# Second attention of a two-attention transformer block: the value product as three float16 matmuls with a lag of two steps

## The chip, the cores and the metric

The kernel runs on one core of one Trainium2 chip. The metric is device microseconds of one execution, as the median of repeated runs. TensorE is called PE here, its weight loads PEld, VectorE DVE, ScalarE ACT, GpSimd POOL.

## The reference, cut to what matters

A sequence of 2048 tokens with 128 channels passes through an attention with 16 heads of 64, a feed-forward block, a second attention with 8 heads of 128 (rotary positions, causal mask) and a second feed-forward block, each behind a layer norm and added to the stream. The change is in the second attention:

```
q = _rope(einsum('btm,mhd->bthd', x, w_aq));  k = _rope(einsum(..., w_ak));  v = einsum(..., w_av)
s = einsum('bihd,bjhd->bhij', q, k) / 128 - 1e30 * mask        # mask: i < j
p = softmax(s, axis=-1)
o = einsum('bhij,bjhd->bihd', p, v)
r = einsum('bihd,hdm->bim', o, w_ao)
```

## The kernel before

Every engine has a program of its own, written out by hand; semaphores tie them. An engine works strictly in its own order, so the order of each program sets everything.

**The second attention.** For each of the 8 heads, queries are taken in 4 units of 512 (qb = 0 to 3; below, unit 0 to unit 3). Unit qb has 4(qb+1) steps of 128 keys, so a head has 4 + 8 + 12 + 16 = 40 steps. The last four steps of a unit lie on the diagonal and have 512, 384, 256 and 128 query columns. Two heads make one turn of a loop; the first and the last turn are written out.

**One step on PE** (`body_b`): three matmuls of keys by queries with 512 columns (L1459, L1461, L1463; high and low parts of q and k) onto a PSUM bank that ACT has filled with minus the row maximum; then a first ring item; then `pv_b` of the step before: up to four value products (query tiles 0 and 1, a second ring item, query tiles 2 and 3), each one float32 matmul of 129 columns (128 values and a column of ones, L1436); then the remaining ring items. The score banks are two, `SB[step % 2]`.

**Ring items** are all other PE work: two PSUM banks `RING`, used in turn. PE may write item n only when DVE has taken item n-2 (`claim`). Kinds: `max` (a score matmul for the row maximum of a later unit, L1389, taken by DVE with a reduction, L855), `rows` and `spread` (bring the maxima into place), `project` (q or k of the next head, L1369; DVE takes it with three multiplications, L1021 to L1023), `values` (V of the next head, L1377; DVE copies it, L1040), `turned` (transpose of the normalised output of the unit before, L1206) and `output` (its product with the output weights, L1214). In unit 3 a `project` stands in steps 1, 3, 5 and 8; in unit 1 in step 5; in unit 2 in steps 3, 6 and 9. In unit 2, steps 0 to 7 have two `max` items each, and `values` stand in steps 4, 7 and 10.

**ACT** per step: wait for the scores, exponential into `PRB` (L719), copy minus the maxima into the score bank for step + 2 (`fill`, L700); one step after a `project`, the rounded high part of q or k (L689), which waits for POOL's sum.

**POOL**: for each `project` a sum (`rope_sum_b`, L512) once DVE has taken it, then the low part (`low_b`, L519) once ACT has the high part. Otherwise it is idle here.

**DVE**: takes ring items in their order; in step 1 of a unit, ahead of that step's items, it normalises the unit before (`normalise_b`, L1030 to L1034), which needs that unit's last value product. `turned` in step 2 waits on PE for this (`o_taken`).

The first attention has the same skeleton; its value products are already pairs of 16-bit matmuls of 194 and 130 columns (L1247, L1248) whose low part of P is made by POOL (L449).

## Time and profile before

| | |
|---|---|
| three runs | 2596.69, 2598.87, 2598.98 us (median 2598.87) |
| span of the profiled execution | 2594.6 us; the page gives no other time for it |
| mean granted PE clock over the span | 0.975 |
| first attention, about | 55 to 1725 us of the span |
| second attention | 1827 to 2547 us, 720 us, 90 us a head |
| busy share over the span | PE 92%, PEld 73%, DVE 68%, ACT 67%, POOL 57% |

How to read it: the span runs from the first to the last instruction of the profiled execution. A matmul's record ends with its modelled pipeline, well after the next one has started. What PE spends on a matmul is therefore read from one start to the next, not from its duration, and PE's busy share hides short waits.

### The profile page before, as it was taken

To read this page: it belongs to the slowest core of one execution; us is meant where nothing else is said; L and a number is where in the kernel's file an instruction comes from. 1 tells how busy PE (TensorE), PEld (TensorE's weight loads), DVE (VectorE), ACT (ScalarE), POOL (GpSimd) and SP (SyncE) were. 2 spreads that over 40 slices of the span, in tenths; PEclk is the share of its full clock that TensorE was granted. 3 is DMA by queue.
4 is the path that set the end of the run, shared out by engine and by line. 5 is a ranking of instruction groups with operands and counts; after the bars stand their busy time and mean duration, and the time that the engine had idled before them with its cause. 6 is when DMAs were issued, how large, how long until landed. Compare 5 with 4: busy or idle time off the path is not lost.

```text
span 2594.6 us, 47816 instructions
## 1 busy us (share of the span) xinstructions
PE 2390.6 (92%) x17315; PEld 1882.8 (73%) x17315; DVE 1769.3 (68%) x3012; ACT 1732.4 (67%) x2190; POOL 1469.7 (57%) x826
## 2 busy tenths in 40 slices
PE   5999999999899899989989999977899999999998
PEld 3777777677777677767767777754788887888786
DVE  6777767677677677767776777666666665666652
ACT  4877877778688687777878878752455454455554
POOL 5787777677687677767777777753122112122200
PEclk7999999999999999999999999988899999999999
DMA  3000000000000000000000000010000000000000
GB/s 94 1 1 1 1 1 1 2 1 1 2 1 1 2 1 1 2 2 1 1 2 1 1 1 1 1 41 1 1 1 1 1 1 2 1 1 1 1 1 17
DMA packets 15276, 13.06 MB, mean 5 GB/s; under 512 B 3120, under 2 KB 14384, under 8 KB 14768
## 3 DMA queue, kind: packets, MB, share of 16 engines
q1 hardware_dynamic: 15024, 9.72, 1.4%
q8 instruction: 156, 2.56, 0.4%
q14 instruction: 96, 0.79, 0.1%
HBM read 8.67 MB, written 1.05 MB: 4 GB/s over the span
## 4 chain that ended last, share of the span: by engine, by line
PE 46%; issue 26%; DVE 13%; POOL 9%; ACT 4%; SPq 0%; DMA 0%; DVEq 0%; POOLq 0%; ACTq 0%
PE OO L1247 6%; PE RING L1193 6%; PE ST L1297 5%; POOL PAB L449 5%; PE ST L1298 5%; DVE maxes L855 4%; PE OO L1248 4%; PE OO L1436 3%; DVE OSUM L889 2%; PE RING L1214 2%; POOL F L512 2%; PE RING L1173 2%; PE RING L1389 1%; PE ST L1459 1%; ACT PAB L636 1%
## 5 line engine op out<-in xcount | busy, mean ns | idle before, releaser
L449 POOL TENSOR_TENSOR PAB<-PR,PAB 128x1024 f16<-128x1024 f32 x512 | 1093.2, 2137 | 407.8 <-ACT PAB L636 390.1
L855 DVE TENSOR_REDUCE maxes<-RING 128x1 f32<-128x512 f32 (+1 forms) x1344 | 883.9, 670 | 417.4 <-PE RING L1193 294.1
L634 ACT ACTIVATE PR<-ST,lift 128x1024 f32<-128x1024 f32 x512 | 569.1, 1111 | 360.0 <-PE ST L1298 354.0
L1247 PE MATMUL OO<-VP,PAB 128*128 128x194 bf16 x4096 | 688.3, 250 | 5.5 <-POOL PAB L449 2.0
L1248 PE MATMUL OO<-VP,PAB 128*128 128x130 bf16 x4096 | 653.3, 220 | 0.0
L636 ACT ACTIVATE PAB<-ST,lift 128x1024 f16<-128x1024 f32 x512 | 565.8, 1105 | 0.0
L1247 PEld LDWEIGHTS OO<-VP,PAB 128*128 128x128 f16 x4096 | 400.7, 98 | 190.4 <-issue 127.1
L1193 PE MATMUL RING<-KH,QL 128*128 128x512 f32 x1024 | 457.0, 453 | 46.4 <-DVE maxes L855 39.7
L1297 PE MATMUL ST<-QL,KH 128*128 128x512 f32 x1024 | 453.9, 443 | 29.2 <-issue 13.7
L1248 PEld LDWEIGHTS OO<-VP,PAB 128*128 128x128 f16 x4096 | 403.7, 99 | 10.8 <-issue 9.9
L1298 PE MATMUL ST<-QH,KL 128*128 128x512 f32 x1024 | 405.6, 396 | 0.0
L512 POOL TENSOR_TENSOR F<-F,PR 128x512 f32<-128x512 f32 x64 | 81.4, 1272 | 508.9 <-DVE PR L1023 508.9
L719 ACT ACTIVATE PR<-ST 128x512 f32<-128x512 f32 (+1 forms) x320 | 169.4, 529 | 260.5 <-PE ST L1463 258.5
L1193 PEld LDWEIGHTS RING<-KH,QL 128*128 128x128 f32 x1024 | 196.1, 192 | 139.0 <-DVE maxes L855 117.8
L1436 PEld LDWEIGHTS OO<-PAB,PR 128*128 128x128 f32 x1536 | 227.4, 192 | 41.1 <-issue 22.7
L1436 PE MATMUL OO<-PAB,PR 128*128 128x129 f32 x1536 | 250.7, 280 | 0.0
L1297 PEld LDWEIGHTS ST<-QL,KH 128*128 128x128 f32 x1024 | 195.5, 191 | 66.4 <-issue 38.7
L1298 PEld LDWEIGHTS ST<-QH,KL 128*128 128x128 f32 x1024 | 195.9, 191 | 33.0 <-issue 7.2
L700 ACT ACTIVATE ST<-VF 128x512 f32<-128x512 f32 (+1 forms) x320 | 172.0, 538 | 26.7 <-PE ST L1425 15.3
L1459 PE MATMUL ST<-QH,KH 128*128 128x512 f32 (+1 forms) x320 | 146.3, 457 | 1.0
L1389 PE MATMUL RING<-KH,QH 128*128 128x512 f32 (+2 forms) x320 | 129.3, 408 | 14.7 <-ACT PR L719 8.1
L831 DVE TENSOR_TENSOR KL<-F,KH 64x512 fp32r<-64x512 f32 x64 | 120.5, 1882 | 24.5 <-ACT KH L594 24.0
(132 smaller groups left out, 3044.4 us busy)
## 6 DMA issues: line engine op xcount, KB each, us to landing
X<-in_L_attn_a_x SPq DMA_DIRECT2D x4, 256.0 KB, 4.3
SHARED<-in_rope_cos SPq DMA_DIRECT2D x1, 1024.0 KB, 4.9
SHARED<-in_rope_sin SPq DMA_DIRECT2D x1, 1024.0 KB, 7.1
out<-X SPq DMA_DIRECT2D x4, 256.0 KB, 2.3
RAW<-in_L_attn_a_Wq SPq DMA_DIRECT2D x1, 512.0 KB, 7.5
RAW<-in_L_attn_a_Wk SPq DMA_DIRECT2D x1, 512.0 KB, 7.8
RAW<-in_L_attn_a_Wv SPq DMA_DIRECT2D x1, 512.0 KB, 5.7
RAW<-in_L_attn_a_Wo SPq DMA_DIRECT2D x1, 512.0 KB, 6.8
```

The lines of the kernel that those rows point to most:

```text
L449: pool.tensor_tensor(PB[:, s, :], PR[:, step % 2, :], PA[:, s, :], ALU.subtract).then_inc(p_low_pool, 1)
L634: act.activation(PR[:, step % 2, :], ST[step % 2][:, :], ACT.Exp, bias=lift[:, :])
L636: act.activation(PA[:, step % SLOTS_A, :], ST[step % 2][:, :], ACT.Exp, bias=lift[:, :]).then_inc(sa.exps, 1)
L700: act.activation(SB[parity][:, c0:BLK], MB[:, slot, c0:BLK], ACT.Copy).then_inc(sbb.filled, 1)
L855: dve.reduce_max(maxes[:, qt, c:c + 1], bank[:, 0:width], X_AXIS).then_inc(s.ring_taken, 1)
L1193: pe.matmul(bank[:, :], QL[hs][:, at:at + P], KH[hs][:, c * BLK:(c + 1) * BLK], start=True, stop=True).then_inc(sa.ring_put, 1)
L1247: pe.matmul(o, high, v, start=(m == 0 and qt % 2 == 0), stop=False, skip_group_check=True)
L1248: ins = pe.matmul(o[:, 0:V3_AT], low, v[:, 0:V3_AT], start=False, stop=(m == TILES - 1), skip_group_check=True)
L1297: pe.matmul(tile, KH[hs][:, keys], QL[hs][:, q], start=True, stop=False)
L1298: ins = pe.matmul(tile, KL[hs][:, keys], QH[hs][:, q], start=False, stop=True)
L1436: ins = pe.matmul(bank[:, at:at + VB], PRB[:, step % 2, qt * P:(qt + 1) * P], VBS[:, ul // BLOCKS, step, :], start=(step == 0 and qt in (0 ...
L1459: pe.matmul(tile, KH[hs][:, keys], QH[hs][:, q], start=False, stop=False, skip_group_check=True)
```

## The change

P and V are each split into a float16 high part and a float16 low part, and one float32 value product becomes three float16 matmuls: P high by V high (129 columns), P high by V low (128), P low by V high (129). ACT computes the exponential twice, once in float32 (`PRB`) and once in float16 (`PBH`, four slots). POOL subtracts the two to get the low part (`p_low_part`). `pv_b` now runs two steps behind the scores, and waits for POOL. With it, DVE's `normalise_b` moves from step 1 to step 2 of a unit, while `turned` stays in step 2. DVE takes `values` with two operations, the second waiting for the first. In POOL's program `low_b` of a `project` stands two steps later, ahead of that step's `p_low_part`. Outside the second attention: V is scaled by a power of two from a bound on its size (two POOL products and two DVE sums at the head of the first attention, a chain of seven small DVE operations and one product on POOL behind it), and the maxima are raised by a constant. Cut to its core:

```diff
@@ -73,6 +74,9 @@
 VB = DB + 1
+VSTEP = DB + 2
+SLOTS_B = 4
+LAG_B = 2
 ITER_B = HB // 2
@@ -154,11 +159,13 @@
             items += [("rows", target)]
-    if not (first and ul == 0):
-        items += [("turned",)] if step == 2 else [("output",)] if step == 3 else []
+    if step == LAG_B + 1 and not (first and ul == 0):
+        items += [("output",)]
     if next_head:
         items += [("project", b) for b in PROJECT_B.get((qb, step), [])]
         items += [("values", VALUES_B[qb, step])] if (qb, step) in VALUES_B else []
+    if step == LAG_B and not (first and ul == 0):
+        items += [("turned",)]
     return items
@@ -524,21 +552,36 @@
                     low_b(0, j, j)
+            pool.wait_ge(vscale_ready, 2)
+            pool.tensor_scalar(WAO, WAO, vdown[:, 0:1], None, ALU.mult).then_inc(ones_set, 1)
             pool.wait_ge(x_ready, BLOCKS)
-            pool.memset(VBS[:, :, :, DB:VB], 1.0).then_inc(ones_set, 1)
+            pool.memset(VBH[:, :, :, DB:VB], 1.0).then_inc(ones_set, 1)
+
+            def p_low_part(step, c0, g):
+
+                pool.wait_ge(sbb.exps, g + 1)
+                wait(pool, sbb.pv, g - SLOTS_B + 1)
+                s = step % SLOTS_B
+                pool.tensor_tensor(PBL[:, s, c0:BLK], PRB[:, step % 2, c0:BLK], PBH[:, s, c0:BLK], ALU.subtract
+                                   ).then_inc(p_low_b, 1)
             def heads_b(it, first=False, last=False):
                 k = SKIP if first else 0
+                g = it * G_B
                 for ul in range(UNITS_B):
                     hs, qb = divmod(ul, BLOCKS)
                     head = it * 2 + hs + 1
                     if qb == 0 and not (last and hs == 1):
                         stage_b(1 - hs, head)
                     for step in range(steps_b(qb)):
+                        for item in ring_items_b(ul, step - 2, first, last) if step >= 2 else []:
+                            if item[0] == "project":
+                                low_b(1 - hs, item[1], head * 2 * BLOCKS + item[1])
+                        p_low_part(step, max(0, step - BT * qb) * P, g)
+                        g = g + 1
                         for item in ring_items_b(ul, step, first, last):
                             if item[0] == "project":
                                 rope_sum_b(item[1], LEAD_B - SKIP + it * RING_B + k)
-                                low_b(1 - hs, item[1], head * 2 * BLOCKS + item[1])
                             k += 1
@@ -715,8 +758,11 @@
                         act.wait_ge(sbb.scores, g + 1)
-                        wait(act, sbb.pv, g - 1)
+                        wait(act, p_low_b, g - 1)
                         act.activation(PRB[:, step % 2, c0:BLK], SB[step % 2][:, c0:BLK], ACT.Exp,
+                                       scale=1.0 / DB)
+                        wait(act, sbb.pv, g - SLOTS_B + 1)
+                        act.activation(PBH[:, step % SLOTS_B, c0:BLK], SB[step % 2][:, c0:BLK], ACT.Exp,
                                        scale=1.0 / DB).then_inc(sbb.exps, 1)
@@ -856,9 +903,10 @@
                     link(dve.tensor_reduce(negmax[:, :], maxes[:, :, 0:chunks], X_AXIS, ALU.max, negate=True))
-                    link(dve.tensor_copy(negparts[:, 0:BT].bitcast(F32R), negmax[:, :]))
-                    dve.tensor_tensor(negparts[:, BT:AUX], negmax[:, :], negparts[:, 0:BT],
-                                      ALU.subtract).then_inc(s.max_ready, 1)
+                    raised = LIFT_B if s is sbb else 0.0
+                    link(dve.tensor_scalar(negparts[:, 0:BT].bitcast(F32R), negmax[:, :], raised, None, ALU.add))
+                    dve.scalar_tensor_tensor(negparts[:, BT:AUX], negmax[:, :], raised, negparts[:, 0:BT],
+                                             ALU.add, ALU.subtract).then_inc(s.max_ready, 1)
@@ -1002,6 +1053,17 @@
             normalise_settled(7)
+            dve.wait_ge(vtotal_put, 1)
+            link(dve.tensor_copy(vbound[:, :], O[1][:, 0:2]))
+            link(dve.tensor_tensor(vbound[:, 0:1], vbound[:, 0:1], vbound[:, 1:2], ALU.add))
+            link(dve.tensor_scalar(vbound[:, 0:1], vbound[:, 0:1], float(P), 1e-30, ALU.mult, ALU.max))
+            link(dve.tensor_scalar(vexp[:, :].bitcast(I32), vbound[:, 0:1].bitcast(I32), 1, 0x7F800000,
+                                   ALU.arith_shift_right, ALU.bitwise_and))
+            dve.tensor_scalar(vup[:, :].bitcast(I32), vexp[:, :].bitcast(I32), -1.0, float(204 << 23),
+                              ALU.mult, ALU.add).then_inc(vscale_ready, 1)
+            dve.tensor_scalar(vdown[:, :].bitcast(I32), vexp[:, :].bitcast(I32), 1.0, float(50 << 23),
+                              ALU.mult, ALU.add).then_inc(vscale_ready, 1)
+            dve.wait_ge(vscale_ready, 2)
@@ -1037,8 +1099,11 @@
                 dve.wait_ge(sbb.ring_put, item + 1)
-                dve.tensor_copy(VBS[:, hs, part * BT:(part + 1) * BT, 0:DB],
-                                bank[:, :].rearrange("p (t c) -> p t c", c=DB)).then_inc(sbb.ring_taken, 1)
+                v = bank[:, :].rearrange("p (t c) -> p t c", c=DB)
+                high = VBH[:, hs, part * BT:(part + 1) * BT, 0:DB]
+                link(dve.tensor_scalar(high, v, vup[:, 0:1], None, ALU.mult))
+                dve.scalar_tensor_tensor(VBL[:, hs, part * BT:(part + 1) * BT, :], v, vup[:, 0:1], high,
+                                         ALU.mult, ALU.subtract).then_inc(sbb.ring_taken, 1)
@@ -1082,7 +1147,7 @@
                     for step in range(steps_b(qb)):
-                        if step == 1 and not (first and ul == 0):
+                        if step == LAG_B and not (first and ul == 0):
                             normalise_b((ul - 1) % UNITS_B, done)
@@ -1424,17 +1492,22 @@
             ins.then_inc(sbb.primed, 1)
-            pe.wait_ge(ones_set, 2)
+            pe.wait_ge(ones_set, 3)
             def pv_b(ul, step, g, half):
                 qb = ul % BLOCKS
+                hs = ul // BLOCKS
                 if half == 0:
-                    pe.wait_ge(sbb.exps, g + 1)
+                    pe.wait_ge(p_low_b, g + 1)
                 for qt in range(max(2 * half, step - BT * qb), 2 * half + 2):
                     bank, at = (OB[ul % 2][0], qt * VB) if qt < 3 else (OB[ul % 2][1], 0)
-                    ins = pe.matmul(bank[:, at:at + VB], PRB[:, step % 2, qt * P:(qt + 1) * P],
-                                    VBS[:, ul // BLOCKS, step, :], start=(step == 0 and qt in (0, 3)),
+                    high, low = (p[:, step % SLOTS_B, qt * P:(qt + 1) * P] for p in (PBH, PBL))
+                    pe.matmul(bank[:, at:at + VB], high, VBH[:, hs, step, 0:VB],
+                              start=(step == 0 and qt in (0, 3)), stop=False, skip_group_check=True)
+                    pe.matmul(bank[:, at:at + DB], high, VBL[:, hs, step, :], start=False, stop=False,
+                              skip_group_check=True)
+                    ins = pe.matmul(bank[:, at:at + VB], low, VBH[:, hs, step, 0:VB], start=False,
                                     stop=(step == BT * qb + qt), skip_group_check=True)
@@ -1493,14 +1566,14 @@
                         ring_items(1)
-                        if not (first and ul == 0 and step == 0):
-                            pul = ul if step else (ul - 1) % UNITS_B
-                            pstep = step - 1 if step else steps_b(pul % BLOCKS) - 1
-                            if step == 1:
+                        if not (first and ul == 0 and step < LAG_B):
+                            pul = ul if step >= LAG_B else (ul - 1) % UNITS_B
+                            pstep = step - LAG_B if step >= LAG_B else steps_b(pul % BLOCKS) + step - LAG_B
+                            if step == LAG_B:
                                 wait(pe, sbb.o_taken, u - 1)
-                            pv_b(pul, pstep, g - 1, 0)
+                            pv_b(pul, pstep, g - LAG_B, 0)
                             ring_items(1)
-                            pv_b(pul, pstep, g - 1, 1)
+                            pv_b(pul, pstep, g - LAG_B, 1)
                         ring_items(len(items) - place)
```

How rows move, at the start of unit 3 of the first head. On PE, before, from the `project` of step 1 (L1369) to the end of step 2. L1436 into OO or ST1 is a value product, L1459 to L1463 are the scores, L1388 and L1389 the `max`, L1206 `turned`:

```order
L1369 MATMUL RING1<-XNT,WST 128x512
L1436 MATMUL OO<-PAB,PR 128x129 x3
L1436 MATMUL ST1<-PAB,PR 128x129
L1459 MATMUL ST0<-QH0,KH0 128x512
L1461 MATMUL ST0<-QH0,KL0 128x512
L1463 MATMUL ST0<-QL0,KH0 128x512
L1388 MATMUL RING0<-later_keys,ident_r 128x128
L1389 MATMUL RING0<-KH1,QH1 128x128
L1436 MATMUL OO<-PAB,PR 128x129 x2
L1206 MATMUL RING1<-ident,AB 128x128 x4
```

and after, the same place from the `project` (L1437) on. L1506, L1508, L1510 are one value product, L1532 to L1536 the scores, L1456 and L1457 the `max`:

```order
L1437 MATMUL RING1<-XNT,WST 128x512
L1506 MATMUL ST1<-PAB,VP 128x129
L1508 MATMUL ST1<-PAB,VP 128x128
L1510 MATMUL ST1<-PAB,VP 128x129
L1532 MATMUL ST0<-QH0,KH0 128x512
L1534 MATMUL ST0<-QH0,KL0 128x512
L1536 MATMUL ST0<-QL0,KH0 128x512
L1456 MATMUL RING0<-later_keys,ident_r 128x128
L1457 MATMUL RING0<-KH1,QH1 128x128
```

The last value product of unit 2 (into ST1), which stood ahead of the scores of step 1, now stands behind them and behind the `project`. Two value products and `turned` (now L1271) follow as before.

On DVE, at the same place, before: `values` (L1040), `normalise_b` (L1030 to L1034), the `project` of step 1, `max`, `turned` (L872):

```order
L1040 COPY PAB<-RING1 128x4x128
L1030 RECIPROCAL rden<-OO 128x3
L1031 RECIPROCAL rden<-ST1 128x1
L1032 TENSOR_TENSOR AB<-OO,rden 128x384
L1034 TENSOR_SCALAR AB<-ST1,rden 128x128
L1021 TENSOR_TENSOR F<-RING1,SHARED 128x512
L1022 TENSOR_TENSOR PR<-RING1,SHARED 64x512
L1023 TENSOR_TENSOR PR<-RING1,SHARED 64x512
L855 TENSOR_REDUCE maxes<-RING0 128x1
L872 COPY AT<-RING1 128x512
```

and after:

```order
L1104 TENSOR_SCALAR PAB<-RING0,vup 128x4x128
L1105 SCALAR_TENSOR_TENSOR PAB<-RING0,vup,PAB 128x512
L1083 TENSOR_TENSOR F<-RING1,SHARED 128x512
L1084 TENSOR_TENSOR PR<-RING1,SHARED 64x512
L1085 TENSOR_TENSOR PR<-RING1,SHARED 64x512
L1092 RECIPROCAL rden<-OO 128x3
L1093 RECIPROCAL rden<-ST1 128x1
L1094 TENSOR_TENSOR AB<-OO,rden 128x384
L1096 TENSOR_SCALAR AB<-ST1,rden 128x128
L902 TENSOR_REDUCE maxes<-RING0 128x1
L920 COPY AT<-RING1 128x512
```

The normalisation now stands behind the `project` instead of ahead of it, and `values` are two operations.

## Rows read from the trace of the kernel before

**Rows 1.** Stretch, length, busy us of PE, PEld, DVE, ACT, POOL, clock, DMA share, GB/s.

```profile
100.00:1690.00 1590.00, 1495.49 (x11692) 1148.07 (x11692) 1145.98 (x1724) 1234.54 (x1320) 1202.39 (x618) 0.99 0.01 1
1827.00:2547.00 720.00, 687.62 (x4456) 589.34 (x4455) 450.45 (x857) 370.43 (x694) 146.37 (x124) 0.99 0.00 1
```

**Rows 2.** PE timeline, second attention: start, duration (us), operation, count; two records a product.

```profile
2000.47 0.83 PE L1436 MATMUL OO<-PAB,PR 128*128 128x129 f32 x6
2001.14 0.39 PE L1436 MATMUL ST<-PAB,PR 128*128 128x129 f32 x2
2001.29 0.47 PE L1459 MATMUL ST<-QH,KH 128*128 128x512 f32 x1
2001.60 0.39 PE L1461 MATMUL ST<-QH,KL 128*128 128x512 f32 x1
2001.82 0.39 PE L1463 MATMUL ST<-QL,KH 128*128 128x512 f32 x1
```

**Rows 3.** PE timeline, first attention: pairs of 16-bit matmuls around a score matmul.

```profile
1200.11 0.25 PE L1247 MATMUL OO<-VP,PAB 128*128 128x194 bf16 x1
1200.20 0.22 PE L1248 MATMUL OO<-VP,PAB 128*128 128x130 bf16 x1
1200.25 0.25 PE L1247 MATMUL OO<-VP,PAB 128*128 128x194 bf16 x1
1200.34 0.22 PE L1248 MATMUL OO<-VP,PAB 128*128 128x130 bf16 x1
1200.37 0.47 PE L1193 MATMUL RING<-KH,QL 128*128 128x512 f32 x1
1200.68 0.26 PE L1247 MATMUL OO<-VP,PAB 128*128 128x194 bf16 x1
```

**Rows 4.** DVE timeline, unit 3, start: normalisation, taking the `project`, `max`.

```profile
1976.64 0.18 DVE L1030 RECIPROCAL rden<-OO 128x3 f32<-128x3 f32 x1 [2.03 <-PE ST L1436]
1977.38 0.34 DVE L1034 TENSOR_SCALAR AB<-ST,rden 128x128 f32<-128x128 f32 x1
1978.60 0.69 DVE L1021 TENSOR_TENSOR F<-RING,SHARED 128x512 f32<-128x512 f32 x1 [0.87 <-PE RING L1369]
1980.72 0.29 DVE L855 TENSOR_REDUCE maxes<-RING 128x1 f32<-128x128 f32 x1
```

**Rows 5.** PE timeline, same stretch: `project` and `turned`.

```profile
1977.54 1.02 PE L1369 MATMUL RING<-XNT,WST 128*128 128x512 f32 x2
1980.75 0.66 PE L1206 MATMUL RING<-ident,AB 128*128 128x128 f32 x4
```

**Rows 6.** ACT timeline where a `project` is followed by short steps (idle before, releaser).

```profile
1944.06 0.63 ACT L689 ACTIVATE QH<-F 128x512 fp32r<-128x512 f32 x1 [1.57 <-POOL F L512]
1945.43 0.58 ACT L719 ACTIVATE PR<-ST 128x512 f32<-128x512 f32 x1
1946.04 0.60 ACT L700 ACTIVATE ST<-VF 128x512 f32<-128x512 f32 x1
1946.58 0.58 ACT L719 ACTIVATE PR<-ST 128x512 f32<-128x512 f32 x1
```

**Rows 7.** PE timeline, unit 2: the second `max` behind a `project`.

```profile
1956.34 0.50 PE L1389 MATMUL RING<-KH,QH 128*128 128x512 f32 x1 [0.82 <-DVE PR L1023]
```

**Rows 8.** POOL groups: low part of P, first attention; sum, second attention (busy us, mean ns).

```profile
L449 POOL TENSOR_TENSOR PAB<-PR,PAB 128x1024 f16<-128x1024 f32 x486 | 1037.8, 2137 | 386.8 <-ACT PAB L636 369.3 <-PE OO L1248 17.4
L512 POOL TENSOR_TENSOR F<-F,PR 128x512 f32<-128x512 f32 x52 | 66.2, 1274 | 405.7 <-DVE PR L1023 405.7
```

**Rows 9.** DVE groups: `values` in the second attention; L860 in first, then second attention.

```profile
L1040 DVE COPY PAB<-RING 128x512 f32<-128x512 f32 x25 | 17.3, 692 | 8.1 <-PE RING L1377 7.6
L860 DVE TENSOR_TENSOR negparts<-negmax,negparts 128x4 f32<-128x4 f32 x61 | 53.5, 878 | 2.1
L860 DVE TENSOR_TENSOR negparts<-negmax,negparts 128x4 f32<-128x4 f32 x27 | 4.4, 163 | 0.9
```

**Rows 10.** The page's group of 16-bit weight loads, first attention (busy us, mean ns).

```profile
L1248 PEld LDWEIGHTS OO<-VP,PAB 128*128 128x128 f16 x4096 | 403.7, 99 | 10.8 <-issue 9.9
```

More of the change, by code:

```diff
@@ L87 @@
 AUX = 2 * BT
+LIFT_B = DB * float(np.log(LIFT))
 def steps_b(qb):
@@ L232, in build @@
         rden = sb("rden", [P, BT])
+        ones_f = sb("ones_f", [P, P])
+        vsum = sb("vsum", [P, 2])
+        vbound = sb("vbound", [P, 2])
+        vexp = sb("vexp", [P, 1])
+        vup = sb("vup", [P, 1])
+        vdown = sb("vdown", [P, 1])
         KH = [sb(f"KH{i}", [P, T], F32R) for i in range(2)]
@@ L298, in build @@
         wt_put = sem("wt_put")
+        squared = sem("squared")
+        vsum_ready = sem("vsum_ready")
+        vtotal_put = sem("vtotal_put")
+        vscale_ready = sem("vscale_ready")
+        p_low_b = sem("p_low_b")
         wt_act = sem("wt_act")
@@ L1324, in _ @@
             output(sa, RING[(END_A - 1) % 2], END_A - 1, WoT[:, ITER_A - 1, :])
+            pe.wait_ge(vsum_ready, 1)
+            pe.matmul(O[1][:, 0:2], ones_f[:, :], vsum[:, :], start=True, stop=True).then_inc(vtotal_put, 1)
             pe.wait_ge(sa.ring_taken, END_A)
@@ L1511, in _ @@
             k = body_b(ITER_B - 1, last=True)
-            for half in range(2):
-                pv_b(UNITS_B - 1, TILES - 1, ITER_B * G_B - 1, half)
+            for step in range(TILES - LAG_B, TILES):
+                for half in range(2):
+                    pv_b(UNITS_B - 1, step, ITER_B * G_B - TILES + step, half)
             n = LEAD_B - SKIP + (ITER_B - 1) * RING_B + k
```

19 lines of the change are left out of this document (17 added, 2 removed).

## The prediction

> **What bounds the kernel now.** I began with the busy time by stretch. In the second attention, 720 of the 2594.6 us, PE is busy 687.6 us, DVE 450, ACT 370 and POOL 146 [rows 1]: PE is nearly full and POOL, where the new work goes, is nearly empty. That speaks for the change. But a matmul's record ends late, so PE's busy time hides short waits, and I read PE's timeline from start to start. Three value products take 2001.14 - 2000.47 = 0.67 us, 0.223 us each; a score matmul takes 0.22 to 0.23 us [rows 2]. A full step is then 3 x 0.227 + 4 x 0.223 = 1.57 us plus ring items. With all items so counted (`project` 0.86 us from [rows 5] to the next start; `turned`, `output` and `values` by the same float32 rate of 0.11 us for 128 columns), a head comes to about 83 us, where the trace has 720 / 8 = 90 [rows 1]. So some 7 us a head are already waits, in three kinds: PE for DVE behind a `project` (0.82 us in [rows 7]); ACT for POOL's sum (1.57 us in [rows 6]) and PE then for ACT; and the turn of the loop. PE waits there for an order, not for throughput, and a faster product shortens none of it.
>
> **The products.** The program of the changed kernel has 136 products a head, 1088 in all. The nearest row for the new kind is the first attention's pair of 194 and 130 columns, 0.14 us from start to start (1200.11 to 1200.25), of which the 130 columns take 0.05 to 0.06 (1200.20 to 1200.25) [rows 3]. Three of 129, 128 and 129 columns come to 3 x 0.057 = 0.171 us. Saved: 0.052 x 1088 = 56.6 us. Against it stands the end of each run of such matmuls: the float32 score matmul behind it takes 1200.68 - 1200.37 = 0.31 us and the last 16-bit one 0.03, together 0.34 where 0.057 + 0.227 = 0.284 would be due: 0.06 lost [rows 3]. Before, the same place costs nothing: the last record of a product begins at about 2001.26, the second next score matmul at 2001.60, 0.34 us for 0.11 + 0.23 [rows 2]. A ring item splits the products of most steps, so there are 58 runs a head, 464: 27.8 us lost. Net for PE: **-28.7 us**. Bounds: -56.6 if the loss vanishes; the other end is the rival on weight loads below.
>
> **The transpose that waits.** `normalise_b` moves to step 2, and `turned`, which needs it, stays there. Worked out at unit 3 of the profiled head. PE begins the `project` of step 1 at 1977.54 [rows 5] and would be through with it at 1978.40, with the one product behind it (0.23) at 1978.63, the scores of step 2 (0.68) at 1979.31, the `max` (0.29) at 1979.60, two products (0.40) at 1980.0: there `turned` is due. DVE takes the `project` from 1978.60 to 1980.7, and only then normalises, which took 1976.64 to 1977.72, 1.08 us [rows 4]: 1981.8. `turned` waits 1.8 us; before it began at 1980.75 [rows 5] with no wait for the normalisation, which was over. I take 1.7. In unit 1, DVE still has two `max` of 0.69 when step 2 begins, then 1.08, then the `max` whose bank `turned` needs: 0.9 us of wait, 0.7 more than now. In units 0 and 2 the same count gives 0.5 and 0.3. While PE waits, all that stands behind it waits: the remaining products, the scores of step 3 and so ACT and POOL. 1.5 us in eight heads and 1.7 in seven (the last head has no `project`): **+23.5 us**. Bounds: 0 if DVE runs ahead everywhere, 30 if all four waits are as in unit 3's arithmetic without overlap.
>
> **ACT.** Each step gets a second exponential. From exponential to fill 0.61 us, from fill to the next exponential 0.54 (1945.43, 1946.04, 1946.58) [rows 6]; two exponentials in a row overlap, so a full step costs 0.54 + 0.61 + 0.54 = 1.69 us. Where ring items stand, PE needs 1.6 to 2.9, and ACT hides. In the last head's unit 3 there are none: PE would need 0.68 + 4 x 0.171 + 0.06 = 1.42, ACT 1.69 for 12 steps: the 1.7 us counted as saved there are not, and 0.7 come on top: +2.4. The last two products of all then wait for two exponentials and POOL: +0.8. Behind the `project` of unit 1 the steps are short and ACT, held by POOL's sum until 1944.06 [rows 6], then has 1.69 us of work a step to catch up with instead of 1.15; but the lag of two gives 1.1 us back. +0.2 a head, 1.5. Together **+4.7**.
>
> **POOL.** 512 columns of `p_low_part` cost half of 2137 ns, 1.07 us; the two operations for a `project` 1.27 each [rows 8]. In unit 3, steps 3 to 7, POOL has five of the one and five of the other (sum and low part for steps 3 and 5, and the low part of step 5 at step 7): 5.4 + 6.4 = 11.7 us; PE needs 10.9. The sum also stands ahead of the next `p_low_part` and itself waits for DVE. Followed row by row from the end of step 3: the low part for step 5 is ready at 6.9 us, PE wants it at 6.5; that for step 6 at 9.2, PE wants it at 8.7. 0.95 us a head, seven heads: **+6.6**. Elsewhere POOL hides in PE's longer steps. What it costs if that cover goes is the third rival.
>
> **DVE.** `values` cost 0.69 us [rows 9] and become two such operations. PE reaches the second `max` behind them 1.3 us after handing them over, DVE is ready after 1.6: 0.3. In unit 2 they also hold `rows` and so `spread`: 0.5. With seven heads 5.6; ahead of the first head four of them stand one behind another with nothing else: +3. Further, L860 took 878 ns in the first attention, where POOL is busy 1202 of 1590 us, and 163 ns in the second, where POOL is idle [rows 1, 9]. POOL will now be busy there about 500 us, so four times a head up to half a microsecond comes back; in unit 3, step 15, and unit 1, step 4, PE waits for it: +0.3 a head, 2. Together **+10.6**. The Trainium skill (SBUF — State Buffer, section "Who interferes with whom") says that a VectorE instruction with two SBUF inputs contends with a GpSimd instruction that reads SBUF, and that the loser blocks; the rows on L860 agree. By that rule most DVE work here, which reads PSUM, stays free, and the term stays as small as I have it.
>
> **What is free.** The scaling of V: two POOL products and two DVE sums while both wait at the start of the first attention; the seven small operations (0.17 us each) in a DVE pause; no term, and at most 3 us if that cover fails.
>
> **The sum.** -28.7 + 23.5 + 4.7 + 6.6 + 10.6 = +16.7 us. Waits in one unit hide part of one another (while PE waits for `turned`, DVE, ACT and POOL catch up), for which I take 4 off: +13. Against the profiled execution: 2594.6 + 13 = 2607.6. The runs' median is 4.3 above that span, so **2612 us**, 0.5% slower.
>
> **Rivals.**
> *The products win (0.27).* If `turned` waits less than about 10 us in all instead of 23.5, the kernel is faster. For it: DVE is busy only 450 of 720 us, and the lag of two may remove waits of PE for ACT that I left standing. Against: the order in unit 3 is fixed, and [rows 4] leave no slack in it. With half of all my losses: 2598.9 - 28.7 + 20 = 2590; with a quarter 2581.
> *A wash (0.13).* The losses come within 5 us of the gain: 2594 to 2604.
> *POOL sets the pace of unit 3 (0.12).* If `p_low_part` costs 1.27 as its neighbour does [rows 8], nine steps of unit 3 and those behind the `project` items of unit 2 lose 0.2 us each and the late sum makes ACT late too: +3 us a head, 2636.
> *Weight loads pace the products (0.08).* Each new matmul loads its own weights, three loads a product where two stood. A load's record lasts 99 ns [rows 10]; unhidden that is 0.297 us a product, +80 us against now. The pair in 0.14 us with two loads [rows 3] speaks against it but allows 0.07 a load, 0.21 a product: then only 0.013 x 1088 = 14 us are saved, the losses stay, and the time is about 2612 + 28 = 2640. The Trainium skill (TensorE: Matmul & The Clock Gate, "Back-to-back issue gap") gives about 81 ns a matmul for N = 128 in a stream of load and matmul pairs; by it a product would take 0.243 us, more than now. The 0.14 us of [rows 3] for a pair contradict it, and the trace decides.
>
> **Chances and range.** My forecast (2602 to 2628) has 0.40, the rivals 0.27, 0.13, 0.12 and 0.08. Differences within 0.2%, some 5 us, can't be told from none here. Slower: nearly all of 0.40 and the last two, 0.6; same 0.13; faster 0.27. The range leaves out the lowest part of the first rival and the highest of the last two: 2580 to 2642.
>
> **What the new profile would show.** A value product in 0.17 us from start to start, and 0.31 behind each run. `turned` idle for DVE's L1096, 1.5 to 2 us in unit 3. In unit 3's steps 7 and 8, PE waiting for POOL's low part. POOL busy near 500 us of the second attention, ACT near 560. `values` at 1.4 to 1.5 us on DVE. The forecast is wrong if `turned` does not wait, if a product does not take 0.17 us, or if POOL's operation is far from 1.07.

## The result, and the profile after

| | before | after |
|---|---|---|
| median, the two side by side on one chip | 2598.45 us | 2629.08 us (2626.79 to 2630.6, 4 runs) |
| span of the profiled execution | 2594.6 us | 2625.0 us |
| first to last score matmul (L1459; L1532) | 1826.4 to 2546.5 | 1831.7 to 2576.4 |

The ratio is 1.012 (95% interval 1.0106 to 1.0135): 30.6 us slower. Direction and range held; the size did not, since the forecast was 13 us slower. Of the 30.6, 5.3 lie ahead of the first score matmul of the second attention and 24.6 between its first and its last: 720.1 us became 744.7.

The page of the changed kernel, its head and its busy line:

```profile
span 2625.0 us, 51188 instructions
PE 2374.8 (90%) x18405; PEld 1812.0 (69%) x18405; DVE 1817.3 (69%) x3053; ACT 1862.5 (71%) x2510; POOL 1792.5 (68%) x1149
```

Its busy time in the two stretches that answer to [rows 1] (same columns):

```profile
100.00:1690.00 1590.00, 1495.71 (x11671) 1147.79 (x11670) 1144.22 (x1722) 1233.95 (x1319) 1201.30 (x618) 0.99 0.01 1
1832.00:2577.00 745.00, 665.89 (x5536) 514.42 (x5536) 492.60 (x885) 500.90 (x1014) 464.16 (x443) 0.99 0.01 1
```

The first attention is as it was. In the second, PE has 22 us less to do and takes 25 us longer: the time is in waits. PE's timeline at the start of unit 3 of the same head, against [rows 2, 3]:

```profile
1984.88 0.22 PE L1506 MATMUL ST<-PAB,VP 128*128 128x129 f16 x1
1984.94 0.22 PE L1508 MATMUL ST<-PAB,VP 128*128 128x128 f16 x1
1984.99 0.22 PE L1510 MATMUL ST<-PAB,VP 128*128 128x129 f16 x1
1985.02 0.49 PE L1532 MATMUL ST<-QH,KH 128*128 128x512 f32 x1
1985.34 0.40 PE L1534 MATMUL ST<-QH,KL 128*128 128x512 f32 x1
```

From start to start the three matmuls take 0.06, 0.05 and, the last one of the run, 0.03 us, and the score matmul behind them 0.32. That is the forecast's price of a product, and within 0.01 us its price of a run's end. Who waited for whom on PE in the second attention, first before, then after (us in total, times, longest):

```profile
PE RING L1389 <- ACT PR L719: 8.1, 7, 1.3
PE RING L1388 <- DVE PR L1023: 6.0, 7, 0.9
PE RING L1389 <- DVE PR L1023: 5.7, 7, 0.8
PE RING L1200 <- DVE negparts L860: 2.7, 8, 0.4
```

```profile
PE RING L1271 <- DVE AB L1096: 19.1, 13, 2.0
PE RING L1265 <- DVE negparts L908: 15.2, 22, 1.1
PE RING L1457 <- DVE PR L1085: 8.5, 14, 0.9
PE RING L1456 <- DVE PR L1085: 6.7, 7, 1.0
PE RING L1457 <- POOL VP L565: 5.6, 7, 0.9
```

Two waits have grown most. The first is the transpose behind the normalisation, as forecast: 7 of its 13 stand in step 2 of unit 3 (1.95 to 2.04 us each), 6 in step 2 of unit 0 (0.80 to 0.89). The second is `rows` (L1265, before L1200) behind two operations of DVE on four columns, 22 times and 15.2 us where it was 8 times and 2.7: the forecast gave it 2. The groups behind these waits, after (busy us, mean ns):

```profile
L565 POOL TENSOR_TENSOR VP<-PR,VP 128x512 f16<-128x512 f32 x224 | 259.8, 1161 | 149.4 <-ACT VP L765 148.5
L1105 DVE SCALAR_TENSOR_TENSOR PAB<-RING,vup,PAB 128x512 f16<-128x512 f32 x28 | 21.0, 751 | 1.0
L1104 DVE TENSOR_SCALAR PAB<-RING,vup 128x512 f16<-128x512 f32 x28 | 20.9, 748 | 8.5 <-PE RING L1445 8.3
L908 DVE SCALAR_TENSOR_TENSOR negparts<-negmax,negparts 128x4 f32<-128x4 f32 x30 | 19.2, 640 | 1.0
L907 DVE TENSOR_SCALAR negparts<-negmax 128x4 fp32r<-128x4 f32 x30 | 17.3, 577 | 1.0
```

L908 (before L860) went from 163 ns [rows 9] to 640, L907 (before L859) from 170 to 577. They stand one behind the other ahead of `rows`, four times a head, and the means hide where they are slow: in step 8 of unit 2 and step 6 of unit 3 the two take 2.05 us together instead of 0.33, in step 4 of unit 1 0.6, in step 15 of unit 3 still 0.33. Step 8 of unit 2 in the second head, both engines:

```profile
1975.72 0.87 DVE L907 TENSOR_SCALAR negparts<-negmax 128x4 fp32r<-128x4 f32 x1
1976.63 1.18 DVE L908 SCALAR_TENSOR_TENSOR negparts<-negmax,negparts 128x4 f32<-128x4 f32 x1
...
1975.41 1.16 POOL L565 TENSOR_TENSOR VP<-PR,VP 128x512 f16<-128x512 f32 x1
1976.53 1.27 POOL L547 TENSOR_TENSOR QL<-F,QH 128x512 fp32r<-128x512 f32 x1
```

L907 ends at 1976.59, 0.02 us behind POOL's low part of P (L565, until 1976.57), and L908 at 1977.81, 0.01 us behind the low part of a `project` (L547, `low_b`, until 1977.80), which POOL runs right behind it. Each small operation lasts until the POOL instruction beside it is over.

### The profile page after: what moved, and what is told of

It is laid out like the page before. It is cut to its first block, busy times and chain, and to the rows that moved or that the text cites. A ratio compares the mean times of both kernels' runs of the same rounds, so it can differ in the third digit from the quotient of the medians.

```text
span 2625.0 us, 51188 instructions
## 1 busy us (share of the span) xinstructions
PE 2374.8 (90%) x18405; PEld 1812.0 (69%) x18405; DVE 1817.3 (69%) x3053; ACT 1862.5 (71%) x2510; POOL 1792.5 (68%) x1149
## 4 chain that ended last, share of the span: by engine, by line
PE 37%; issue 29%; DVE 14%; POOL 14%; ACT 5%; POOLq 0%; SPq 0%; DMA 0%; DVEq 0%; ACTq 0%
POOL PAB L472 8%; PE RING L1258 5%; PE OO L1312 5%; PE ST L1362 4%; DVE maxes L902 4%; PE ST L1363 4%; PE OO L1313 3%; POOL VP L565 3%; PE RING L1279 1%; ACT PAB L679 1%; PE RING L1457 1%; DVE OSUM L937 1%; PE RING L1246 1%; PE RING L1238 1%; PE ST L1532 1%
## 5 line engine op out<-in xcount | busy, mean ns | idle before, releaser
L902 DVE TENSOR_REDUCE maxes<-RING 128x1 f32<-128x512 f32 (+1 forms) x1344 | 882.1, 670 | 399.0 <-PE RING L1258 294.5
L565 POOL TENSOR_TENSOR VP<-PR,VP 128x512 f16<-128x512 f32 (+1 forms) x320 | 324.2, 1014 | 195.9 <-ACT VP L765 192.6
L765 ACT ACTIVATE VP<-ST 128x512 f16<-128x512 f32 (+1 forms) x320 | 168.4, 526 | 0.0
L1506 PE MATMUL OO<-PAB,VP 128*128 128x129 f16 x768 | 156.0, 226 | 2.8 <-POOL VP L565 2.4
L1510 PE MATMUL OO<-PAB,VP 128*128 128x129 f16 x768 | 152.7, 222 | 0.0
L1508 PE MATMUL OO<-PAB,VP 128*128 128x128 f16 x768 | 152.3, 221 | 0.0
```

The lines of the kernel that those rows point to most:

```text
L565: pool.tensor_tensor(PBL[:, s, c0:BLK], PRB[:, step % 2, c0:BLK], PBH[:, s, c0:BLK], ALU.subtract).then_inc(p_low_b, 1)
L765: act.activation(PBH[:, step % SLOTS_B, c0:BLK], SB[step % 2][:, c0:BLK], ACT.Exp, scale=1.0 / DB).then_inc(sbb.exps, 1)
L902: dve.reduce_max(maxes[:, qt, c:c + 1], bank[:, 0:width], X_AXIS).then_inc(s.ring_taken, 1)
```

## The experiments

Each is an edit of the changed kernel where nothing else is said. Ratios are to the kernel before, which ran on the same chip with each and took 2597.6 to 2598.8 us; after stands for 2629.1. The 95% intervals reach 2 to 4 us either way, so a difference of less than some 3 to 5 us between two edits can't be told from none by the times alone. Where the text speaks of places, the profiled executions were compared step by step, from the first score matmul of one step to that of the next, and summed over the heads. The granted clock also differs between these kernels; the table at the end of this section has what it took from each.

**Normalisation ahead of the `project`, unit 3 only.**

```diff
-                        if step == LAG_B and not (first and ul == 0):
+                        if step == (1 if qb == 3 else LAG_B) and not (first and ul == 0):
```

> In unit 3 alone, DVE normalises the unit before in step 1, ahead of the project, and no longer in step 2 behind it; all else as in the changed kernel (median 2629). Theory A (order: the transpose waits behind the project on DVE): the wait of 2.2 us in unit 3's step 2 falls to some 0.5, seven heads: 2629 - 12 = 2617. Rival B (the same idle time would show up in another wait, since DVE and the shared SBUF port are what is short): within 3 us of 2629.

Measured: 2627.27 us, 1.0116 (1.0099 to 1.0133), 2 us less than after, which can't be told from none: rival B. DVE and PE at the start of unit 3 of this kernel:

```profile
1989.05 0.18 DVE L1092 RECIPROCAL rden<-OO 128x3 f32<-128x3 f32 x1 [3.50 <-PE ST L1510]
1990.05 0.68 DVE L1083 TENSOR_TENSOR F<-RING,SHARED 128x512 f32<-128x512 f32 x1
1991.45 0.68 DVE L1085 TENSOR_TENSOR PR<-RING,SHARED 64x512 f32<-64x512 f32 x1
...
1992.19 0.66 PE L1271 MATMUL RING<-ident,AB 128*128 128x128 f32 x4 [1.90 <-DVE PR L1085]
```

The normalisation is over at 1990.1 and `turned` starts no earlier than in the changed kernel (1992.21, below). It now waits for L1085, DVE's last read of the `project`: `turned` is written to the bank that the `project` filled, two items before. The `project` (2.1 us of DVE) and the normalisation (1.1) fall into the same window with the lag of two, and `turned` needs both; their order hardly matters.

**The two small operations as reductions.**

```diff
+                    if s is sbb:
+                        link(dve.tensor_reduce(negparts[:, 0:BT].bitcast(F32R), maxes[:, :, 0:chunks], X_AXIS,
+                                               ALU.max, negate=True))
+                        dve.tensor_reduce(negmax[:, :], maxes[:, :, 0:chunks], X_AXIS, ALU.max, negate=True
+                                          ).then_inc(s.max_ready, 1)
+                        return
                     link(dve.tensor_scalar(negparts[:, 0:BT].bitcast(F32R), negmax[:, :], raised, None, ALU.add))
```

> In the second attention the two small operations on the row maxima that read SBUF twice or in a fast mode are replaced by reductions of the same length, which do not slow down beside GpSimd; left out are the low part of the maximum and the constant raise. Theory A (these two operations, 0.60 and 0.70 us instead of 0.17 and 0.16, are the mis-sized term, and the rows item waits for them, about 2 us a head): 2629 - 14 = 2615. Rival B (they are slow but DVE's backlog of ring items holds the rows item anyway): 2624 to 2629.

Measured: 2609.87 us, 1.0047 (1.003 to 1.0063), 19 us less than after. A group of each of the two reductions in this kernel (busy us, mean ns), and then the first and last start of its score matmuls:

```profile
L908 DVE TENSOR_REDUCE negparts<-maxes 128x4 fp32r<-128x16 f32 x8 | 1.4, 170 | 0.3
L910 DVE TENSOR_REDUCE negmax<-maxes 128x4 f32<-128x16 f32 x8 | 1.4, 170 | 0.3
```

```profile
L1540 PE MATMUL ST<-QH,KH x320: 274/475/796, 1832.7 to 2560.4; 128*128 128x512 f32 x128, 128*128 128x256 f32 x32
```

The same number of operations, again writing four columns, takes 158 to 170 ns beside the same busy POOL, and the second attention shrinks from 744.7 to 727.7 us. By place, 11.5 us of the 17 are in steps 8 and 9 of unit 2 and 7.1 in steps 6 to 8 of unit 3, and nothing changes in step 4 of unit 1 or step 15 of unit 3 (a lower clock in step 3 of unit 3 takes 1.6 back). The slowing of L907 and L908 is the largest error of the forecast.

**No low part of P.**

```diff
-                pool.wait_ge(sbb.exps, g + 1)
-                wait(pool, sbb.pv, g - SLOTS_B + 1)
-                s = step % SLOTS_B
-                pool.tensor_tensor(PBL[:, s, c0:BLK], PRB[:, step % 2, c0:BLK], PBH[:, s, c0:BLK], ALU.subtract
-                                   ).then_inc(p_low_b, 1)
+                return
...
-                    high, low = (p[:, step % SLOTS_B, qt * P:(qt + 1) * P] for p in (PBH, PBL))
+                    high, low = (p[:, step % SLOTS_B, qt * P:(qt + 1) * P] for p in (PBH, PBH))
```

> GpSimd's subtraction is left out, and the third product uses the high part of P again; PE waits for ACT instead of GpSimd. PE, ACT and DVE have the same instructions as in the changed kernel. Theory A (GpSimd costs twice: by blocking DVE's small operations, 14 us, and by coming late in unit 3 and holding ACT, 8 us): 2629 - 22 = 2607. Rival B (GpSimd costs only by being late): 2621. Rival C (PE waits for DVE's order alone): 2628.

Measured: 2603.74 us, 1.0021 (1.0012 to 1.0031), 25 us less than after. DVE's two small operations, with their original code, in this kernel:

```profile
L903 DVE TENSOR_SCALAR negparts<-negmax 128x4 fp32r<-128x4 f32 x30 | 5.1, 170 | 1.0
L904 DVE SCALAR_TENSOR_TENSOR negparts<-negmax,negparts 128x4 f32<-128x4 f32 x30 | 4.9, 162 | 1.0
```

So it is POOL's new work that slows them (L908, in the rows above, beside `low_b`, which runs right behind the subtraction only in the changed kernel's order). This edit takes away both that and POOL's lateness. The distance to the kernel with reductions is 2609.87 - 2603.74 = 6.1 us. By place, steps 7 and 8 of unit 3 are 6.6 us shorter, where and as much as forecast for the lateness; the rest of the kernel gains 1.7 us in unit 0 and loses 3.2 in steps 2 and 3 of unit 3, where the clock fell (last section). The largest row of waits for POOL, L1457 with 5.6 us, is another matter: it stands in step 0 of unit 2, where the kernel before waited 8.1 us for ACT, and with POOL's part out steps 0 and 1 of unit 2 are no shorter.

**One exponential as well**: the kernel without POOL's low part, and without the float32 exponential too.

> As the kernel without POOL's low part (2603.74), and without the float32 exponential as well: its third value product takes P high by V high a second time. A: the second exponential costs as I counted, about 5 us, mostly in the last head: 2599. B: ACT is hidden everywhere: within 1.5 us of 2603.7. C: ACT with two exponentials paces the steps of unit 3 in every head, and 10 us or more come back: 2594 or less.

Measured: 2602.98 us, 1.0014 (1.0005 to 1.0024), 0.8 us below the one above, which is in B's range. But this kernel loses 3.6 us more to the clock (16.4 against 12.8), so what the second exponential itself costs, with POOL out of the way, lies between 0.8 and some 4.4 us, and the forecast of 4.7 is not refuted. From first to last score matmul the last head, where most of it was put, became 1.1 us shorter.

**The lag alone**: the kernel before, float32 products, with the lag of two and the normalisation in step 2.

```diff
-    if not (first and ul == 0):
-        items += [("turned",)] if step == 2 else [("output",)] if step == 3 else []
+    if step == LAG_B + 1 and not (first and ul == 0):
+        items += [("output",)]
...
-                        if step == 1 and not (first and ul == 0):
+                        if step == LAG_B and not (first and ul == 0):
...
-                            pv_b(pul, pstep, g - 1, 0)
+                            pv_b(pul, pstep, g - LAG_B, 0)
```

> The kernel before with one part of the change: the float32 product two steps behind the scores, four float32 slots for P, DVE's normalisation in step 2. Theory A (the order alone costs the waits of the transpose, 3.5 us a head, less 1 us for waits on ACT that the lag takes away): 2598.5 + 20 = 2618. Rival B (a lag of two by itself costs nothing, the loss comes with GpSimd): 2595 to 2601.

(The kernel also has the four slots for P.) Measured: 2612.21 us, 1.0056 (1.0039 to 1.0073), 14.4 us more than before. Its longest wait on PE (L1211 is `turned`, L1039 the normalisation there):

```profile
PE RING L1211 <- DVE AB L1039: 17.6, 14, 1.9
```

Against it the lag removes waits for ACT: 8.1 and 2.5 us before, 4.3 and 0.8 here.

**One copy of V**: DVE takes `values` with one operation, and the second product uses the high part of V again.

```diff
-                link(dve.tensor_scalar(high, v, vup[:, 0:1], None, ALU.mult))
-                dve.scalar_tensor_tensor(VBL[:, hs, part * BT:(part + 1) * BT, :], v, vup[:, 0:1], high,
-                                         ALU.mult, ALU.subtract).then_inc(sbb.ring_taken, 1)
+                dve.tensor_scalar(high, v, vup[:, 0:1], None, ALU.mult).then_inc(sbb.ring_taken, 1)
```

> The low part of V is left out (one DVE operation on values instead of two; the second product uses the high part again). Theory A (the second operation is on PE's path behind values in unit 2 and ahead of the first head: 0.65 and 0.4 us a head, 3 us once): 2629 - 9 = 2620. Rival B (it hides in DVE's idle time): 2627 to 2630.

Measured: 2622.86 us, 1.0095 (1.0078 to 1.0112), 6.2 us less than after. Its first score matmul starts at 1828.9 where the changed kernel has 1831.7: 2.8 us of it are ahead of the first head (forecast 3). In the heads of the profiled execution steps 5 and 9 of unit 2, behind `values`, are 7.1 us shorter (forecast 5.6), and steps 2 and 3 of unit 3 are 6.4 us longer at a lower clock (the clock takes 15.9 us instead of 9.8). So the second operation cost about 10 us, and the time shows 6.2. (A fourth `values` stands in step 9 of unit 3, where nothing changed.)

**Two products instead of three**: P high by V low left out.

```diff
-                    pe.matmul(bank[:, at:at + DB], high, VBL[:, hs, step, :], start=False, stop=False,
-                              skip_group_check=True)
```

> The product of P high by V low is left out on PE alone: 1088 matmuls of 57 ns less, 62 us of PE's work. Theory A (much of unit 2 and 3 is paced by DVE's chain and PE only waits longer): about half comes back, 2629 - 30 = 2599. Rival B (PE's throughput is still the bound): 2629 - 60 = 2569. Rival C (PE no longer matters): over 2615.

Measured: 2607.38 us, 1.0037 (1.0026 to 1.0048), 21.7 us less than after. The 1088 matmuls left out took 1088 x 0.057 = 62 us of PE. Its busy time in the second attention and four of its waits on PE:

```profile
1832.00:2556.00 724.00, 617.84 (x4442) 457.22 (x4441) 491.15 (x885) 496.87 (x1012) 463.09 (x442) 0.98 0.00 1
```

```profile
PE RING L1265 <- DVE negparts L908: 18.8, 22, 1.1
PE RING L1457 <- DVE PR L1085: 10.9, 14, 1.0
PE OO L1506 <- POOL VP L565: 7.3, 13, 0.6
PE RING L1271 <- DVE maxes L902: 7.1, 16, 0.8
```

A third of what PE saved reached the time. Most of the rest reappears as longer waits for DVE, ACT and POOL (those that the profile lists add up to 104.7 us on PE instead of 78.5), and up to 4.8 us went to the clock.

**`turned` a step later in unit 3** (and `output` with it).

```diff
-    if step == LAG_B + 1 and not (first and ul == 0):
+    late = LAG_B + (qb in (3,))
+    if step == late + 1 and not (first and ul == 0):
         items += [("output",)]
...
-    if step == LAG_B and not (first and ul == 0):
+    if step == late and not (first and ul == 0):
```

> In unit 3 the transpose stands in step 3 instead of 2 and the output product in step 4 instead of 3. Theory A (the transpose needs both the bank of the project and the normalisation, 3.2 us of DVE work in one window, and one step more hides it): its wait of 2.2 us goes, 2629 - 13 = 2616. Rival B (the wait moves to the next item that needs a bank): 2624 to 2629.

Measured: 2614.08 us, 1.0065 (1.0048 to 1.0081), 15 us less than after. `turned` behind the normalisation (L1272, L1097 there) and `rows` (L1266):

```profile
PE RING L1266 <- DVE negparts L909: 9.7, 15, 1.1
PE RING L1272 <- DVE AB L1097: 5.9, 7, 0.9
```

The seven waits of some 2 us are gone; the seven left, up to 0.9 us, are unit 0's. `rows` waits 15 times instead of 22, which the forecast had no word for: moving one item also shifted DVE against POOL, and in step 6 of unit 3 the second small operation (L909 there) now meets an idle POOL and takes 0.16 us instead of 1.19. Unit 3 is 9.5 us shorter in all; most of the other 3.4 us between the first and the last score matmul are the start of the fifth head, where the clock did not fall as it does in the changed kernel.

**Both repairs.** `turned` later in units 1 to 3, and the maxima by four reductions, with which the second part of minus the maximum is kept (the raise is then a bias of the exponentials).

```diff
+                        dve.tensor_reduce(both[:, :, 0], m, X_AXIS, ALU.max, negate=True)
+                        link(dve.tensor_reduce(both[:, :, 1].bitcast(F32R), m, X_AXIS, ALU.max))
+                        link(dve.tensor_reduce(negparts[:, 0:BT].bitcast(F32R), m, X_AXIS, ALU.max, negate=True))
+                        dve.tensor_reduce(negparts[:, BT:AUX], both[:, :, :], X_AXIS, ALU.add
+                                          ).then_inc(s.max_ready, 1)
```

> All of the changed kernel's results are kept. The transpose stands one step later in units 1 to 3, and the row maxima are split by four reductions on DVE instead of one reduction and two operations that slow down beside GpSimd; the raise is a bias of the exponential. Theory A (both waits are separate and add up, 19 and 18 us): 2629 - 37 = 2592, faster than the kernel before (2598). Rival B (they overlap or move on): 2600 to 2608.

Measured: 2602.95 us, 1.0019 (1.001 to 1.0029), 26 us less than after, but 5 more than before: B. With `turned` later in unit 3 alone:

> The transpose later in unit 3 alone, and the two small operations beside POOL made into reductions; the kernel that moved it later in units 1 to 3 took 2602.95. A: the moves in units 1 and 2 gained about what they cost, and the time is 2601 to 2605. B: they only pushed the item into steps that were full (its step 4 of unit 2 took longer), and without them it is 2597 to 2600, no longer to be told from the kernel before.

Measured: 2606.84 us, 1.0029 (1.0019 to 1.004). The moves in units 1 and 2 were worth 3.9 us by the times; by place unit 1 gains 2.5 and unit 2 loses 1.2. B is wrong, and A was 2 us too low. Next, the same move with the edit of the small operations from above, and so without the second part of minus the maximum and without the raise. The expectation calls this two reductions instead of four; it counts the two replaced ones, and with the first reduction, which stays, the kernel has three:

> The same move in unit 3 with the cheaper form of the maxima: the part of minus the maximum that one rounded value can't hold is left out, two reductions instead of four. The two effects apart were -19 and -15 us against the changed kernel. A: they add up, 2595. B: they hide part of one another (what DVE loses in a step is hidden where PE waits for it anyway), 2600 to 2603. The distance to the kernel with four reductions is what the two further ones cost.

Measured: 2599.55 us, 1.0001 (0.9992 to 1.0011). The effects of 19 and 15 us overlap by 4 or 5 by the times, by 1 from first to last score matmul (17.0 and 12.9 us against 28.9). The kernel with four reductions takes 7 us more, but that is not the price of reductions. It has only one more, 0.16 us, and the waits of `rows` are 2.7 us instead of 2.1; its raise is a bias of both exponentials, which makes every one of them longer. The float32 exponential with the bias (L764) and without (L763):

```profile
L764 ACT ACTIVATE PR<-ST,lift 128x512 f32<-128x512 f32 x220 | 149.3, 679 | 84.9 <-PE ST L1546 84.2
L763 ACT ACTIVATE PR<-ST 128x512 f32<-128x512 f32 x224 | 132.0, 589 | 105.9 <-PE ST L1545 105.7
```

PE's waits for ACT's fill are 10.3 us (27 times) with it and 4.5 (12 times) without, and up to 3.5 us of the 7 are the clock. No run has four reductions without the bias, so what a kernel that keeps all results would take is open. Last, the edit of the small operations with `turned` later in units 1 to 3:

> The transpose later in units 1 to 3 and the two-reduction form of the maxima (the second part of minus the maximum left out). Measured: 2599.55 with the move in unit 3 alone; with four reductions the moves in units 1 and 2 were worth 3.9 us (2606.84 to 2602.95). A: the same here, 2595.5 to 2597, 0.1% below the kernel before. B: nothing, 2599 to 2600. If the products were worth their 29 us and nothing else of the change remained but setup, ACT and the values, it would be near 2588; how far it stays above tells what the lag itself still costs.

Measured: 2596.71 us, 0.9995 (0.9986 to 1.0004), A: no different from before. Its first and last score matmuls:

```profile
L1541 PE MATMUL ST<-QH,KH x320: 273/475/796, 1832.4 to 2546.9; 128*128 128x512 f32 x128, 128*128 128x256 f32 x32
```

With both waits mended the second attention takes 714.5 us, 5.6 less than before the change, and about as much is lost ahead of it. That is what is left of the products when the two waits are mended (at the price of the maximum's second part and the raise) and the other costs still stand.

**What the clock took.** PE's granted clock is at the upper of its two levels (2.4 GHz) for most of the second attention and at the lower (1.2 GHz, 0.50) in a few stretches of 2 to 10 us. The table has, for each profiled execution, the length from first to last score matmul and the most that the clock can have cost in it: the length of each stretch of 2 us times what its granted clock was below 1, summed.

| kernel | length, us | clock, us |
|---|---|---|
| before | 720.1 | 9.2 |
| after | 744.7 | 9.8 |
| normalisation ahead | 745.8 | 11.4 |
| two small operations as reductions | 727.7 | 11.5 |
| no low part of P | 722.4 | 12.8 |
| one exponential as well | 720.6 | 16.4 |
| lag alone | 736.4 | 12.5 |
| one copy of V | 743.3 | 15.9 |
| two products | 725.8 | 14.6 |
| `turned` later, unit 3 | 731.8 | 4.7 |
| both repairs, units 1 to 3 | 719.5 | 6.2 |
| both repairs, unit 3 | 722.8 | 9.6 |
| reductions without the second part, unit 3 | 715.8 | 6.1 |
| reductions without the second part, units 1 to 3 | 714.5 | 9.7 |

The change itself hardly moved it (9.2 to 9.8), so the 24.6 us between the first and the last score matmul are not the clock. But differences between edits hold up to 6 us of it.

## Why the prediction was right, and where it was wrong

**The step that failed** is in the DVE term: "so four times a head up to half a microsecond comes back; in unit 3, step 15, and unit 1, step 4, PE waits for it: +0.3 a head, 2." The mechanism, POOL slowing L860, was named; its size was wrong more than ninefold, 19.2 us by the experiment with reductions. It failed in two places. First, it spoke of L860 alone. L859 was read at 170 ns in the second attention and stood in the profile of the first with 252, against 878 for L860, and I left it out; with POOL's subtractions of 128x512 beside it, it rose to 577. Second, the maxima are the head of a chain (`rows`, L915, `spread`, the fill), and of the four places a head where `rows` waits on them the forecast priced the wrong two. It named step 15 of unit 3, where the wait is 0.24 to 0.33 us and was no shorter before, and step 4 of unit 1, where there is none. The waits that grew are in step 8 of unit 2 (0.98 to 1.09 us) and step 6 of unit 3 (0.75 to 0.85), and the reductions took them away there. One of them, in unit 2, behind the two operations shown above:

```profile
1977.96 0.27 PE L1265 MATMUL RING<-ident,negparts 128*8 128x128 f32 x1 [1.09 <-DVE negparts L908]
```

The Trainium skill (SBUF — State Buffer, "Who interferes with whom") had more to say than I used. I took only its rule on two SBUF inputs, which covers L860 and not L859. It also says that `tensor_scalar` and copies can enter a mode that takes the pair of ports shared with GpSimd, when their operands meet certain conditions, and that `tensor_reduce` never contends on trn2. The runs agree: the `tensor_scalar` L907 took 577 ns beside POOL's subtractions and 170 without them, the reductions 158 to 170 beside them. Which mode L907 ran in no run shows.

**The products** took 0.17 us each and 0.06 at a run's end, as forecast. That their -28.7 would reach the time was the second weak step. The prediction says itself that PE waits "for an order, not for throughput, and a faster product shortens none of it", and then subtracts all of it. Of the 62 us in the experiment with two products a third came through. The removals add up to 14.4 (lag) + 19.2 (small operations) + 6.1 (POOL) + 0.8 (ACT) + 6.2 (values) + 2.6 (start, below) = 49.3; against +30.6 this leaves about -19 for the products. It is a remainder over effects that overlap and over clocks that differ by some us, and no run measured it alone.

**The transpose that waits**: +23.5 less 4 for overlap (its own factors, 1.5 in eight heads and 1.7 in seven, give 23.9). Measured 1.96 us in unit 3, where 1.7 was forecast, and 0.89 in unit 0, where it was 0.5. The second row below is step 2 of unit 0:

```profile
1992.21 0.63 PE L1271 MATMUL RING<-ident,AB 128*128 128x128 f32 x4 [1.96 <-DVE AB L1096]
...
2027.84 0.63 PE L1271 MATMUL RING<-ident,AB 128*128 128x128 f32 x4 [0.89 <-DVE AB L1096]
```

In unit 1, forecast at 0.9, it is 0.39 to 0.46 and for the bank of a `max` (L902), and in unit 2 the profile lists none. The sum of the waits, 19.1 + 3.3 = 22.4 us, is near the forecast because the errors by unit offset one another. To the time it brought less: 14.4 us by the lag alone, which also took away 5.5 us of waits for ACT, and 15 by moving the item in unit 3, of which 5.8 are the wait of `rows` behind it and up to 5 the clock. In unit 3 the place was right; the cause was half of it, since the bank of the `project` holds `turned` just as long.

**POOL**: 1.16 us instead of 1.07 for 512 columns, and 6.6 us in steps 7 and 8 of unit 3, size and place as forecast. **ACT**: between 0.8 and some 4.4 us instead of 4.7, measured only with POOL's part out. **Values**: about 10 us by place instead of 8.6. **What is free**: the scaling of V was not quite. Before the four `values` DVE is already 2.6 us late (it begins to take a `project` ahead of the first head at 1797.49, before at 1794.93). 1 us of it is there at 39 us; another part comes at 54 us, where L908 takes 0.95 instead of 0.30 us (L860) while POOL makes the two products for the bound:

```profile
54.05 0.95 DVE L908 SCALAR_TENSOR_TENSOR negparts<-negmax,negparts 128x4 f32<-128x4 f32 x1
...
53.94 1.04 POOL L490 TENSOR_TENSOR AT<-RAW 128x512 f32<-128x512 f32 x1
```

Where the remaining 1 us arises was not traced. **The rivals**: weight loads did not pace the products (0.057 us a matmul), POOL did not pace unit 3, and the products did not win. The price of the rival on weight loads does not follow from its own numbers: with 14 us saved instead of 56.6 and the losses unchanged it is 2612 + 43, not 2612 + 28.

## What to carry to other kernels

When an idle engine gets steady work, list every instruction of the other engines that is slower in a stage where that engine is already busy (here L859 with 252 against 170 ns and L860 with 878 against 163), the tiny ones above all, and follow who waits for them: two operations on four columns cost more here than the 1.16 us subtractions beside them did by being late. Time saved on an engine that often waits for an order is worth a fraction of itself, here about a third, so find that fraction before subtracting it. Before crediting a few us to an edit, compare the granted clocks of the two executions. And when one step of a pipeline lags further, count how much work of the serving engine falls between the last use of a bank and the next item, for each bank, not only for the data.

## What was not expected of the hardware

In the kernel without POOL's low part, PE's granted clock fell by half after the wait of 1.96 us for `turned` in unit 3. Its busy time and clock in three stretches behind the wait (columns as in [rows 1]):

```profile
1988.30:1989.50 1.20, 1.20 (x11) 1.14 (x10) 0.52 (x1) 0.54 (x1) 0.59 (x1) 0.52 0.00 0
1989.50:1990.50 1.00, 1.00 (x4) 0.81 (x4) 0.17 (x1) 0.00 (x0) 0.69 (x1) 0.50 0.00 0
1990.50:1992.50 2.00, 2.00 (x16) 1.81 (x15) 0.42 (x1) 1.46 (x3) 0.00 (x0) 0.68 0.04 8
```

The clock is at the lower of its two levels (1.2 GHz, 0.50 to 0.52) until about 1991.7 and back at the upper behind it. At the same wait of the same head the changed kernel (1.96 us) and the one with one exponential less (1.95) kept the upper level; but the latter fell in four other heads at this place, the kernel without POOL's low part in three of seven, the one with one copy of V in four, the changed kernel in none, and the six kernels without a wait of 2 us there, before and those with `turned` later, in none. What decides between them stays open, but a wait of some 2 us on PE can cost more than its own length. From the start of `turned` to the start of `output` it took 1991.82 - 1988.09 = 3.73 us here and 1990.88 - 1988.75 = 2.13 in the kernel with one exponential less: 1.6 us.

The other surprise is that an operation on 128x4 elements, 0.16 to 0.17 us alone, takes up to 1.19 us beside POOL's operations on 128x512 (1.16 and 1.27 us each), and ends when they end: the delay does not shrink with the size of the operation that is delayed. DVE's operations that read PSUM kept their times beside the same POOL, `values` with 748 and 751 ns against 751 and 751 without its subtractions, the last one of the normalisation with 342 against 342.
